# Storing finished chunks one by one and loading the next batches into their place

## Chip, cores and metric

One Trainium2 chip, one core of it. The metric is the device time of the kernel in microseconds, the median of several runs. The engines are PE (matmul), DVE (vector), ACT (scalar), POOL (general) and SP, which here issues every DMA, on one queue and in order.

## What is computed

The input `x` has 8 batches of 2048 nodes with 64 features; `adj` is a 2048 x 2048 row-normalised adjacency. Four layers follow each other, each with a residual sum and a layer normalisation over the 64 features:

```python
x = _layernorm(x + _L0_gnn_ref(x, adj, embedding, weight, bias))  # Chebyshev, K = 3, weights per node
x = _layernorm(x + _L1_gnn_ref(x, 0, net_params, adj))            # two times relu((A z) W)
x = _layernorm(x + _L2_gnn_ref(x, adj, w_self, w_neighbor, bias)) # x Ws + (A x) Wn + b
x = _layernorm(x + _L3_gnn_ref(x, adj, adj, weight, bias))        # x0, A x0, 2A(A x0)-x0, twice, then W
```

## The kernel before

**Pairs and lanes.** The 8 batches are handled as four pairs, j = 0 to 3. A pair lies in SBUF as a tensor of 128 partitions x 2048, in four chunks (c) of 512 columns. There is room for two pairs, `nat0` and `nat1`: even pairs use lane 0, odd pairs lane 1. `stg0` and `stg1` hold a second tensor of each lane, `ring` the short-lived ones, `td` is scratch in HBM.

**Passes.** A pair goes through seven products with the adjacency, passes p = 0 to 6. Passes 0 and 1 and the per-node weights are layer 0, passes 2 and 3 layer 1, pass 4 layer 2, passes 5 and 6 layer 3. Before a pass, each of its four chunks is split into a high and a low part (step `split`: ACT line 790 makes the high part, DVE line 916 the low one), since PE multiplies both (lines 652 and 653) with `B`, the adjacency's pattern. One chunk of a pass is four quarters (steps `mm`, k = 0 to 3), each of eight matmuls of 128x512. Quarter k of every chunk needs the split of chunk k of the whole tensor. After a chunk, DVE scales it (line 904), PE multiplies it with small weights (`pe_weighed`, line 670), DVE adds it to `nat` (line 945), and in passes 3, 4 and 6 the chunk is normalised (steps `centre`, `deviate`, `normed`; the last instruction of `normed` is line 965).

**Turnings.** In passes 4 and 5 a chunk must be transposed in blocks. DVE transposes within blocks (step `turn`, line 928), SP stores the result to `td` (line 1119), waits until it has landed, and loads it in another order with four DMAs (step `back`, line 1129). With k = 0 it is the tensor that goes to line 670 in that pass, with k = 1 (pass 5) the one that is split for pass 6.

**The order of work.** `order()` writes one list of steps, and every engine runs through that list and does its own part of each step. In the second half of the kernel `lane0` and `lane1` take turns: each gives the other its turn after every chunk, and also once before and once after the splits of a pass. So while one lane is at its splits, the other does up to three chunks of products in a row. Lane 0 does pair 2 and then pair 0, lane 1 pair 3 and then pair 1. Pairs 0, 1 and 2 wait after layer 0 in `zd` in HBM (step `spill`).

**The exchange.** At the end of `second(j, ...)` there are four steps `out` (line 1181), which wait for the chunk's normalisation and store the chunk. `whole_pair` of the next pair in that lane begins with one step `reload`: SP waits for all four stores of the pair before (line 1177), and loads all 2048 columns with one DMA of 1,024 KB (line 1178). Its four splits follow. In the list, `out` of pair 2 stands in pass 5 of pair 3, after the first chunk of that pass; `reload` of pair 0 and its splits stand after the second chunk of it. The exchange of lane 1 stands between pass 2 and pass 3 of pair 0, where nothing is turned. The four stores of pair 0 stand in pass 5 of pair 1, in the same way as those of pair 2.

```python
if s.kind == "reload":
    for i in range(NC):
        sp.wait_ge(s_z[n][i], 32 if j == 2 else 16)
...
    else:
        sp.wait_ge(s_out[n], 64)
    sp.dma_start(nat[n][:], zd[j]).then_inc(s_re[n], 16)
```

A second way through the same steps, for a matrix of another form, is in the program behind a flag and isn't run.

Of the kernel before, what the change touches and what calls it, by code (L numbers as in the profile page):

```python
# [17 lines left out]
NC = 4  # L18
# [16 lines left out]
Step = namedtuple("Step", "kind j p c k", defaults=(0, 0, 0, 0))  # L35
# [7 lines left out]
def order():  # L43
    steps = []

    def put(kind, *at):
        steps.append(Step(kind, *at))

    def one_pass(j, p):

        norm = p in (3, 4, 6)

        def turn(c, k):
            put("turn", j, p, c, k)

        def finish(c):
            put("after", j, p, c)
            if norm:
                if c > 0:
                    put("deviate", j, p, c - 1)  # L60
                put("centre", j, p, c)
                if c > 0:
                    put("normed", j, p, c - 1)

        order = [(c, m) for c in range(NC) for m in range(4)]
        if p == 0 or (j, p) == (2, 2):

            order[0:8] = [(0, 0), (0, 1), (1, 0), (1, 1), (0, 2), (1, 2), (0, 3), (1, 3)]
        for c, m in order:
            if p in (4, 5) and (c, m) == (0, 0):  # L70
                turn(0, 0)
            if p in (4, 5) and (c, m) == (0, 1):
                put("back", j, p, 0, 0)
            if p in (4, 5) and c < 3 and m == 2:
                turn(c + 1, 0)
            if p in (4, 5) and c < 3 and m == 3:
                put("back", j, p, c + 1, 0)
            if p == 5 and c > 0 and m == 1:
                put("back", j, p, c - 1, 1)
            put("mm", j, p, c, m)  # L80
            if c > 0 and p >= 2 and m == (3 if c == 1 and order[2] == (1, 0) else 0):
                finish(c - 1)
            if m < 3:
                yield False
                continue
            if c > 0 and p < 2:
                finish(c - 1)
            put("scale", j, p, c)
            if p == 5 and not on_pe(j, p, c):
                turn(c, 1)  # L90
            if norm and c == 3:
                put("deviate", j, p, 2)
                put("normed", j, p, 2)
            yield True
        put("after", j, p, 3)
        if norm:
            put("centre", j, p, 3)
            put("deviate", j, p, 3)
            put("normed", j, p, 3)

    def opening(j):
        put("prep2", j, 0, 0)
# [56 lines left out]
    def splits(j, p):  # L159
        for c in range(NC):  # L160
            put("split", j, p, c)
# [83 lines left out]
    def second(j, products):  # L245

        for whole in products:
            if whole:
                yield
        for p in (4, 5, 6):  # L250
            yield
            splits(j, p)
            yield
            for whole in one_pass(j, p):
                if whole:
                    yield
        for c in range(NC):
            put("out", j, 0, c)

    def whole_pair(j):  # L260
        if j < 2:
            put("reload", j)
        splits(j, 2)
        yield
        for whole in one_pass(j, 2):
            if whole:
                yield
        yield
        splits(j, 3)
        yield  # L270
        yield from second(j, one_pass(j, 3))
# [32 lines left out]
    n = 0  # L304
    while lanes[0] or lanes[1]:
        if lanes[n] and next(lanes[n], "end") == "end":
            lanes[n] = None
        n = 1 - n
# [3 lines left out]
STEPS = order()  # L312
# [1 line left out]
SECOND = STEPS.index(Step("W"))  # L314


END = STEPS.index(Step("out", 1))


def numbered(*kinds, last=False):  # L320
# [8 lines left out]
def gnn_stack(nc, xn, xt, at, rb, r16, emb, embt, b0, w01, w2, wbd, bias, eye, eps, out, zd, y1d, bd, td):  # L329
# [3 lines left out]
    with ctx:  # L333
# [18 lines left out]
        nat = [sb(f"nat{i}", [P, N], F32) for i in range(2)]  # L352
# [28 lines left out]
        def way(general):  # L381


            def sem(name):
                return ctx.enter_context(nc.semaphore(("g_" if general else "f_") + name))
# [5 lines left out]
            s_lx = [sem(f"loadx{i}") for i in range(2)]  # L391
            s_y1o = [sem(f"y1out{n}") for n in range(2)]
            s_z = [[sem(f"z{n}{c}") for c in range(NC)] for n in range(2)]
            s_re = [sem(f"reload{n}") for n in range(2)]
            s_out = [sem(f"out{n}") for n in range(2)]
            s_away = [sem(f"away{n}") for n in range(2)]
            s_back = [[sem(f"back{n}{k}") for k in range(2)] for n in range(2)]
# [5 lines left out]
            s_hi, s_evict, s_sq, s_std, s_H, s_S, s_twh = (  # L403
                sem("hi"), sem("evict"), sem("sq"), sem("std"), sem("H"), sem("S"), sem("twh"))

            s_lo, s_y, s_v, s_turn = sem("lo"), sem("y"), sem("v"), sem("turn")
# [22 lines left out]
            split_at = numbered("split")  # L429
# [24 lines left out]
            for s in STEPS:  # L454
                if s.kind == "fetch" or s.kind == "part" and s.c == 1:
                    i = s.p if s.kind == "fetch" else 1
                    n_load[i] += 32 if s.kind == "fetch" else 16
                    load_at[s], load_after[s], slot_of[s] = n_load[i], held[i], i
                    held[i] = s

            def turned(j, p, c):

# [52 lines left out]
            for s in STEPS:  # L515
                n = s.j % 2
# [28 lines left out]
            for s in STEPS:  # L545
                n = s.j % 2
# [19 lines left out]
            def ch(t, c):  # L566
                return t[:, c * 512:(c + 1) * 512]
# [61 lines left out]
            def source_of(j, p, c):  # L629

                n = j % 2
                if p == 0 and j < 2:
                    return ch(nat[n], c), s_x[c], 32
                if p == 0:
                    if c == 1:
                        return part_slot(c), s_f[1], load_at[Step("part", j, 0, c)]
                    return part_slot(c), s_p, part_at[Step("part", j, 0, c)]
                if p == 1:
                    return ch(nat[n], c), *((s_evict, evict_at[after(j, 0, c)]) if on_pe(j, 0, c) else landed(j, 0, c, 1))
                if p == 2 and j < 2:  # L640
                    return ch(nat[n], c), s_re[n], 16 * (2 - n)
                if p == 3:
                    return ch(nat[n] if j == 2 else stg[n], c), s_evict, evict_at[after(j, 2, c)]
                if p == 6:
                    return ch(stg[n], c), *((s_evict, evict_at[after(j, 5, c)]) if on_pe(j, 5, c) else landed(j, 5, c, 1))
                return ch(nat[n], c), s_norm, norm_at[Step("normed", j, {2: 1, 4: 3, 5: 4}[p], c)]
# [222 lines left out]
            def dve_steps(dv, steps):  # L869
                for s in steps:  # L870
# [58 lines left out]
                    if s.kind == "after" and p > 2:  # L929
                        dv.wait_ge(s_four, four_at[s])  # L930
                        bank = ps[:, nbank_of[s, "four"], :]
                        if p == 3:
                            if j == 3:
                                dv.wait_ge(s_norm, norm_at[Step("normed", 3, 1, c)])
                                dv.wait_ge(s_hi, split_at[Step("split", 3, 2, c)])
                            else:
                                dv.wait_ge(s_re[n], 32 if j == 0 else 16)
                                dv.wait_ge(s_hi, split_at[Step("split", j, 3 if j == 2 else 2, c)])
                            dv.scalar_tensor_tensor(v, bank, 0.0, v, ALU.max, ALU.add).then_inc(s_v, 1)
                        else:  # L940
                            if p == 6:
                                dv.wait_ge(s_v, v_at[after(j, 5, c)])
                            else:
                                dv.wait_ge(s_pb, pb_at[s])
                            dv.tensor_tensor(v, bank, v, ALU.add).then_inc(s_v, 1)  # L945
# [127 lines left out]
            def sp_settle(sp):  # L1073

                sp.wait_ge(s_here, 4)
                for n in range(2):
                    sp.wait_ge(s_out[n], 128 - 64 * n)

            def sp_rest(sp, c, v):
                for m in range(NT):  # L1080
# [17 lines left out]
            def sp_steps(sp, steps):  # L1098
                for s in steps:
# [67 lines left out]
                    if s.kind == "spill":  # L1167
                        sp.wait_ge(s_norm, norm_at[Step("normed", j, 1, c)])
                        sp.dma_start(zd[j, :, cols], ch(nat[n], c)).then_inc(s_z[n][c], 16)
                    if s.kind == "reload":  # L1170
                        for i in range(NC):
                            sp.wait_ge(s_z[n][i], 32 if j == 2 else 16)
                        if j == 2:
                            sp.wait_ge(s_hi, split_at[Step("split", 2, 3, 3)])
                            sp.wait_ge(s_lo, split_at[Step("split", 2, 3, 3)])
                        else:
                            sp.wait_ge(s_out[n], 64)
                        sp.dma_start(nat[n][:], zd[j]).then_inc(s_re[n], 16)
                    if s.kind == "out":
                        sp.wait_ge(s_norm, norm_at[Step("normed", j, 6, c)])  # L1180
                        sp.dma_start(out[j, :, cols], ch(nat[n], c)).then_inc(s_out[n], 16)
                    if s.kind == "W":
                        sp.wait_ge(s_acc, 8 * n_T)
                        sp.wait_ge(s_H, len(prep_at))
# [1 line left out]
                        sp.dma_start(W[:], wbd[:, 2:9, :]).then_inc(s_w, 16)  # L1186
                    if s == STEPS[-1]:
                        for n in range(2):
                            sp.wait_ge(s_out[n], 128)

            return Way(pe_steps, act_steps, dve_steps, pool_steps, sp_steps,
                       *((act_start, dve_start, sp_start) if general else (None, None, sp_settle)))
# [102 lines left out]
```

## Time and profile before

| | us |
|---|---|
| median of 3 runs | 1267.96 |
| lowest and highest of them | 1266.08, 1274.63 |
| the profiled execution | 1270.8 |
| its span | 1268.7 |

The rows further below come from this profiled execution. A row of a timeline has the start and the duration in us, the engine, the line, the operation with what it writes and reads, and in brackets how long the engine was idle before it and what ended that. "x4" means four instructions merged in one row, so that the duration is from the first one's start to the last one's end. Line numbers are those of the kernel before. Names such as `nat` and `ring` stand without their number.

### The profile page before, as it was taken

What the parts mean: (1) busy time and instruction counts of PE and PEld (TensorE: products, weight loads), DVE (VectorE), ACT (ScalarE), POOL (GpSimd) and SP (SyncE); (2) the same over time, 40 slices, a digit from 0 to 9 for tenths busy, and PEclk for the clock granted to TensorE, in tenths of its full rate; (3) what the DMA queues carried; (4) which work ended last, traced back from release to release, by engine and by line L of the source; (5) the groups of instructions that cost most, each with busy time, mean ns of one, the idle gap of its engine ahead of it and who ended that gap; (6) DMA issues with size and microseconds to landing.
All of it is one profiled execution on the core that took longest, in us unless ns stands there. A gap on an engine that the chain in (4) does not pass through costs nothing.

```text
span 1268.7 us, 16356 instructions
## 1 busy us (share of the span) xinstructions
PE 1232.3 (97%) x5872; PEld 1030.6 (81%) x5872; DVE 758.6 (60%) x1863; ACT 215.5 (17%) x392; POOL 62.0 (5%) x52
## 2 busy tenths in 40 slices
PE   7999999999999999999999999997999999999996
PEld 6888888788878887878888888886888888888875
DVE  5826897787777777788725654542146355544624
ACT  6622111121112101110111111100111111110110
POOL 0000000000000000000000001010000000010100
PEclk9999999999999999999999999998999999999998
DMA  9732112211111111110011143033001110330320
GB/s 346 318 100 59 38 49 64 71 50 42 46 51 62 39 38 38 30 50 13 15 34 34 30 88 67 1 98 85 1 18 50 34 34 25 84 67 9 92 59 35
DMA packets 127783, 78.16 MB, mean 62 GB/s; under 512 B 97217, under 2 KB 107969, under 8 KB 125633
## 3 DMA queue, kind: packets, MB, share of 16 engines
q1 hardware_dynamic: 127696, 77.04, 20.6%
q8 instruction: 50, 0.82, 0.3%
q14 instruction: 37, 0.30, 0.1%
HBM read 53.42 MB, written 23.59 MB: 61 GB/s over the span
## 4 chain that ended last, share of the span: by engine, by line
PE 86%; DVE 6%; DMA 3%; SPq 2%; issue 1%; ACT 1%; DVEq 0%; ACTq 0%
PE ps L652 27%; PE ps L653 27%; PE ps L756 20%; PE ps L670 7%; PE ps L691 2%; PE ps L692 2%; SPq L1129 2%; DVE nat L1018 1%; DVE ring L1018 1%; DMA td<-ring 1%; DMA raw<-in_at 1%; PE ps L664 1%; DVE xs L916 1%; DMA td<-stg 1%; DMA nat<-zd 1%
## 5 line engine op out<-in xcount | busy, mean ns | idle before, releaser
L652 PE MATMUL ps<-B,xs 128*128 128x512 f32 x1664 | 657.1, 395 | 12.2 <-DVE xs L916 12.2
L653 PE MATMUL ps<-B,xs 128*128 128x512 f32 x1664 | 650.4, 391 | 0.0
L652 PEld LDWEIGHTS ps<-B,xs 128*128 128x128 f32 x1664 | 313.6, 188 | 76.7 <-issue 10.0
L653 PEld LDWEIGHTS ps<-B,xs 128*128 128x128 f32 x1664 | 313.9, 189 | 62.4
L756 PE MATMUL ps<-Tw,xs 128*128 128x512 f32 x1280 | 309.4, 391 | 2.5 <-DVE ring L1018 2.5
L756 PEld LDWEIGHTS ps<-Tw,xs 128*128 128x128 f32 x1280 | 238.6, 188 | 55.0 <-DVE ring L1018 4.8
L904 DVE TENSOR_TENSOR ring<-ps,rrep 128x512 f32<-128x512 f32 x94 | 64.5, 689 | 245.9 <-PE ps L653 236.0
L1018 DVE SCALAR_TENSOR_TENSOR nat<-ps,embn,nat 128x128 f32<-128x128 f32 x448 | 154.0, 344 | 51.0 <-PE ps L756 50.7
L1018 DVE SCALAR_TENSOR_TENSOR ring<-ps,embn,ring 128x128 f32<-128x128 f32 x512 | 175.5, 343 | 0.0
L670 PEld LDWEIGHTS ps<-W,ring 128*128 128x128 f32 x896 | 111.6, 191 | 10.6 <-DVE ring L904 3.7
L670 PE MATMUL ps<-W,ring 128*128 128x128 f32 x896 | 113.3, 275 | 2.8 <-DVE ring L904 2.4
L945 DVE TENSOR_TENSOR nat<-ps,nat 128x512 f32<-128x512 f32 x48 | 33.1, 689 | 59.5 <-PE ps L670 59.3
L1044 POOL TENSOR_TENSOR nat<-nat,bias 128x512 f32<-128x512 f32 x32 | 41.2, 1296 | 556.7 <-DVE ring L928 556.7
L916 DVE TENSOR_TENSOR xs<-nat,xs 128x512 fp32r<-128x512 f32 x72 | 45.6, 684 | 30.9 <-ACT xs L790 30.6
L826 ACT ACTIVATE sml<-sml,epst 128x8 f32<-128x8 f32 x64 | 19.3, 301 | 234.7 <-DVE sml L960 234.7
L821 ACT ACTIVATE ps<-nat 128x512 f32<-128x512 f32 x44 | 26.5, 602 | 183.3 <-DVE nat L955 183.3
L691 PE MATMUL ps<-B,xs 128*128 128x512 f32 x128 | 52.3, 409 | 3.4 <-DVE B L878 3.4
L692 PE MATMUL ps<-B,xs 128*128 128x512 f32 x128 | 51.7, 404 | 0.0
L1018 DVE SCALAR_TENSOR_TENSOR nat<-ps,embn,ring 128x128 f32<-128x128 f32 x64 | 22.3, 348 | 46.7 <-PE ps L756 45.9
L1037 POOL TENSOR_TENSOR nat<-nat,ring 128x512 f32<-128x512 f32 x16 | 20.6, 1290 | 588.1 <-DVE ring L1018 588.1
L790 ACT CAST xs<-nat 128x512 fp32r<-128x512 f32 x72 | 39.7, 616 | 37.5 <-DMA nat<-zd 24.4
L955 DVE TENSOR_TENSOR nat<-nat,sml 128x512 f32<-128x512 f32 x64 | 44.4, 693 | 2.2
(66 smaller groups left out, 547.6 us busy)
## 6 DMA issues: line engine op xcount, KB each, us to landing
raw<-in_at SPq DMA_DIRECT2D x13, 1024.0 KB, 16.1
td<-ring SPq DMA_DIRECT2D x32, 256.0 KB, 2.1
ring<-td SPq DMA_DIRECT2D x128, 64.0 KB, 2.5
ring<-in_xn SPq DMA_DIRECT2D x16, 256.0 KB, 2.8
ring_x<-in_xt SPq DMA_DIRECT2D x32, 128.0 KB, 3.2
ring_x<-y1d SPq DMA_DIRECT2D x32, 128.0 KB, 3.3
out<-nat SPq DMA_DIRECT2D x16, 256.0 KB, 2.8
y1d<-ring SPq DMA_DIRECT2D x14, 256.0 KB, 2.7
```

Source lines behind the costliest of these rows:

```text
L652: pe.matmul(bank, x[:, 0, m, :], of, start=m == 0, stop=False)
L653: mm = pe.matmul(bank, x[:, 1, m, :], of, start=False, stop=ends and m == NT - 1)
L670: mm = pe.matmul(ps[:, bank, k * P:(k + 1) * P], src[:, k * P:(k + 1) * P], w, start=i == 0, stop=i == len(pairs) - 1)
L691: pe.matmul(bank, xs[n][:, 0, k, :], of, start=k == 0, stop=False)
L692: mm = pe.matmul(bank, xs[n][:, 1, k, :], of, start=False, stop=k == LAST)
L756: mm = pe.matmul(ps[:, 4 + 2 * p + q, :], src, Tw[:, wi, 512 * p:512 * p + 512], start=i == 0, stop=i == 4)
L790: ac.copy(part_of(j, 0, c), src).then_inc(s_hi, 1)
L904: dv.tensor_tensor(to, ps[:, bank_of["prod", j, p, c], :], ch(rrep, 0 if general else c), ALU.mult).then_inc(s_y, 1)
L916: dv.tensor_tensor(lo, src, hi.bitcast(F32), ALU.subtract).then_inc(s_lo, 1)
L955: dv.tensor_tensor(g, g, sm[:, 1, :].unsqueeze(2).to_broadcast([P, 8, C]), ALU.subtract).then_inc(s_mean, 1)
L1018: dv.scalar_tensor_tensor(sums[d % 2], ps[:, 4 + 2 * p:6 + 2 * p, i * C:(i + 1) * C], embn[:, t, d:d + 1], first[d] if d < 2 else sums[d % 2],
L1044: po.tensor_tensor(g, g, bias_t[:, p - 4, :].unsqueeze(1).to_broadcast([P, 8, C]), ALU.add).then_inc(s_pb, 1)
```

## The change

A store of pairs 0, 2 and 3 is put in the list right behind the normalisation of its chunk (`exchange`), so the first three lie within pass 6 and the fourth at its end. For pairs 2 and 3 each store but the first is followed by the reload of the chunk before it, for the pair that takes the place: 256 KB, which waits for that chunk's store alone. The reload of the fourth chunk stands where the whole reload stood. Of the four splits of pass 2 for pairs 0 and 1 the first three stay, and the fourth moves between the second and the third quarter of that pass's first chunk. Stores and reload pieces of a chunk count on the same semaphore as its `spill` (`exchanged` gives semaphore and count), so that splits and the additions of pass 3 wait for one chunk each. Pair 1's stores stay at the end. The one reload of pair 2 (from its `spill`, earlier in the kernel) is left as it was.

```diff
+        def exchange(c):
+
+            if p == 6 and j != 1:
+                put("out", j, 6, c)
+                if c > 0 and j > 1:
+                    put("reload", j - 2, 0, c - 1)
...
                 if c > 0:
                     put("normed", j, p, c - 1)
+                    exchange(c - 1)
...
+            if p == 2 and j < 2 and (c, m) == (0, 2):
+                put("split", j, 2, 3)
...
                 put("normed", j, p, 2)
+                exchange(2)
...
             put("normed", j, p, 3)
+            exchange(3)
...
-        for c in range(NC):
-            put("out", j, 0, c)
+        if j == 1:
+            for c in range(NC):
+                put("out", j, 6, c)
...
         if j < 2:
-            put("reload", j)
-        splits(j, 2)
+            put("reload", j, 0, 3)
+            for c in range(3):
+                put("split", j, 2, c)
+        else:
+            splits(j, 2)
...
+            def exchanged(j, c, back):
+
+                return s_z[j % 2][c], 16 * (3 - j % 2 + back)
...
                 if p == 2 and j < 2:
-                    return ch(nat[n], c), s_re[n], 16 * (2 - n)
+                    return ch(nat[n], c), *exchanged(j, c, 1)
...
-                                dv.wait_ge(s_re[n], 32 if j == 0 else 16)
+                                dv.wait_ge(*((s_re, 16) if j == 2 else exchanged(j, c, 1)))
...
+                    elif s.kind == "reload":
+                        sp.wait_ge(*exchanged(j + 2, c, 0))
+                        sp.dma_start(ch(nat[n], c), zd[j, :, cols]).then_inc(s_z[n][c], 16)
                     if s.kind == "out":
                         sp.wait_ge(s_norm, norm_at[Step("normed", j, 6, c)])
-                        sp.dma_start(out[j, :, cols], ch(nat[n], c)).then_inc(s_out[n], 16)
+                        sp.dma_start(out[j, :, cols], ch(nat[n], c)).then_inc(s_z[n][c] if j > 1 else s_out[n], 16)
```

On SP, at the exchange of lane 0 during pass 5 of pair 3, before:

```order
L1129 DMA ring<-td 32x16x32 x4
L1119 DMA td<-ring 128x512
L1129 DMA ring<-td 32x16x32 x4
L1119 DMA td<-stg1 128x512
L1181 DMA out<-nat0 128x512 x4
L1129 DMA stg1<-td 32x16x32 x4
L1119 DMA td<-ring 128x512
L1129 DMA ring<-td 32x16x32 x4
L1119 DMA td<-stg1 128x512
L1178 DMA nat0<-zd 128x2048
L1129 DMA stg1<-td 32x16x32 x4
```

and the same place with the change, where a turning's store has become line 1138, a `back` line 1148, a reload piece line 1197 and a store of the output line 1200:

```order
L1200 DMA out<-nat0 128x512 x2
L1197 DMA nat0<-zd 128x512
L1200 DMA out<-nat0 128x512
L1197 DMA nat0<-zd 128x512
L1138 DMA td<-ring 128x512
...
L1138 DMA td<-stg1 128x512
L1200 DMA out<-nat0 128x512
L1197 DMA nat0<-zd 128x512
L1148 DMA stg1<-td 32x16x32 x4
...
L1138 DMA td<-stg1 128x512
L1197 DMA nat0<-zd 128x512
```

Three stores and two pieces went ahead of the first turning of the pass; a store and a piece stand where four stores were; one piece stands where the whole reload was.

On DVE, at the same exchange, before (line 928 is a turning, 916 a split, 945 the addition, 904 the scale):

```order
L904 TENSOR_TENSOR ring<-ps,rrep 128x512
L928 STREAM_TRANSPOSE stg<-ring 128x512
L916 TENSOR_TENSOR xs<-nat,xs 128x512 x4
L945 TENSOR_TENSOR nat<-ps,nat 128x512
L928 STREAM_TRANSPOSE ring<-nat 128x512
L904 TENSOR_TENSOR ring<-ps,rrep 128x512
L928 STREAM_TRANSPOSE stg<-ring 128x512
L904 TENSOR_TENSOR ring<-ps,rrep 128x512
```

and with the change, where these are lines 948, 936, 965 and 924:

```order
L924 TENSOR_TENSOR ring<-ps,rrep 128x512
L948 STREAM_TRANSPOSE stg<-ring 128x512
L936 TENSOR_TENSOR xs<-nat,xs 128x512 x3
L965 TENSOR_TENSOR nat<-ps,nat 128x512
L948 STREAM_TRANSPOSE ring<-nat 128x512
L924 TENSOR_TENSOR ring<-ps,rrep 128x512
L948 STREAM_TRANSPOSE stg<-ring 128x512
L936 TENSOR_TENSOR xs<-nat,xs 128x512
L924 TENSOR_TENSOR ring<-ps,rrep 128x512
```

The fourth split moved behind the addition, the turnings and the scale of lane 1's next chunk.

## Rows read from the trace of the kernel before

**Rows 1.** The page: busy time and share of an engine.
```profile
PE 1232.3 (97%) x5872; PEld 1030.6 (81%) x5872; DVE 758.6 (60%) x1863; ACT 215.5 (17%) x392; POOL 62.0 (5%) x52
```

**Rows 2.** Waits of PE, whole span: us in total, times, longest.
```profile
PE ps L652 <- DVE xs L916: 12.2, 5, 8.0
```

**Rows 3.** Stretches: us, busy of PE, PEld, DVE, ACT, POOL, clock, DMA share, GB/s.
```profile
857.10:865.10 8.00, 0.00 (x0) 0.02 (x1) 0.83 (x2) 1.57 (x4) 0.00 (x0) 0.70 0.70 187
865.10:870.60 5.50, 5.49 (x13) 4.36 (x14) 4.18 (x7) 0.60 (x2) 1.29 (x1) 0.51 0.12 48
960.00:976.00 16.00, 16.00 (x80) 13.56 (x79) 10.96 (x21) 3.99 (x8) 0.00 (x0) 1.00 0.23 83
```

**Rows 4.** Chain that ended last, 825 to 870 us: start, us, what.
```profile
837.04 0.23 PE ps L652
...
845.68 0.46 SPq L1181
...
850.19 2.72 DMA td<-ring
...
856.37 7.13 DMA nat<-zd
863.53 0.63 ACT xs L790
...
864.27 0.70 DVE xs L916
...
865.11 0.77 PE ps L652
865.88 0.43 PE ps L653
```

**Rows 5.** Timeline of SP, lane 0's exchange.
```profile
833.51 0.33 SPq L1119 DMA_DIRECT2D td<-ring  x1
835.64 2.60 SPq L1129 DMA_DIRECT2D ring<-td  x4
...
844.53 0.63 SPq L1119 DMA_DIRECT2D td<-stg  x1
845.21 2.19 SPq L1181 DMA_DIRECT2D out<-nat  x4
847.44 2.71 SPq L1129 DMA_DIRECT2D stg<-td  x4
...
856.37 0.33 SPq L1178 DMA_DIRECT2D nat<-zd  x1
```

**Rows 6.** Timeline of DVE, same stretch.
```profile
832.17 0.69 DVE L965 TENSOR_TENSOR nat<-nat,sml 128x512 f32<-128x512 f32 x1
...
848.81 0.71 DVE L928 STREAM_TRANSPOSE stg<-ring 128x512 f32<-128x512 f32 x1
864.27 2.50 DVE L916 TENSOR_TENSOR xs<-nat,xs 128x512 fp32r<-128x512 f32 x4 [14.76 <-ACT xs L790]
```

**Rows 7.** The page: DMA issues, size of one, median us to landing.
```profile
out<-nat SPq DMA_DIRECT2D x16, 256.0 KB, 2.8
```

**Rows 8.** DMA, 833 to 842 us, in 40 slices.
```profile
GB/s 0 0 0 0 0 27 355 419 346 55 0 0 0 0 0 0 0 12 91 175 23 101 100 84 52 141 74 174 210 346 389 243 73 46 0 0 0 73 0 0
```

**Rows 9.** Timeline of PE: what waited or might have.
```profile
840.55 2.02 PE L670 MATMUL ps<-W,ring 128*128 128x128 f32 x16 [0.34 <-DMA ring<-td]
...
1193.20 2.02 PE L670 MATMUL ps<-W,ring 128*128 128x128 f32 x16
...
1223.75 0.47 PE L652 MATMUL ps<-B,xs 128*128 128x512 f32 x1 [1.47 <-DVE xs L916]
```

**Rows 10.** Timelines of SP and ACT, lane 1's exchange.
```profile
967.32 0.33 SPq L1178 DMA_DIRECT2D nat<-zd  x1
...
972.10 2.18 ACT L790 CAST xs<-nat 128x512 fp32r<-128x512 f32 x4 [3.81 <-DMA nat<-zd]
```

**Rows 11.** Chain that ended last, 1180 to 1224 us: start, us, what.
```profile
1196.38 3.17 DMA td<-stg
```

More of the change, by code:

```diff
@@ L314 @@
 SECOND = STEPS.index(Step("W"))
-END = STEPS.index(Step("out", 1))
+END = STEPS.index(Step("out", 1, 6))
 def numbered(*kinds, last=False):
@@ L393, in way @@
             s_z = [[sem(f"z{n}{c}") for c in range(NC)] for n in range(2)]
-            s_re = [sem(f"reload{n}") for n in range(2)]
+            s_re = sem("reload")
             s_out = [sem(f"out{n}") for n in range(2)]
@@ L1075, in sp_settle @@
                 sp.wait_ge(s_here, 4)
-                for n in range(2):
-                    sp.wait_ge(s_out[n], 128 - 64 * n)
+                sp.wait_ge(s_out[0], 64)
             def sp_rest(sp, c, v):
@@ L1169, in sp_steps @@
                         sp.dma_start(zd[j, :, cols], ch(nat[n], c)).then_inc(s_z[n][c], 16)
-                    if s.kind == "reload":
+                    if s.kind == "reload" and j == 2:
                         for i in range(NC):
[L1172 to L1178, printed above, removed]
+                            sp.wait_ge(s_z[n][i], 32)
+                        sp.wait_ge(s_hi, split_at[Step("split", 2, 3, 3)])
+                        sp.wait_ge(s_lo, split_at[Step("split", 2, 3, 3)])
+                        sp.dma_start(nat[n][:], zd[j]).then_inc(s_re, 16)
+                    elif s.kind == "reload":
+                        sp.wait_ge(*exchanged(j + 2, c, 0))
+                        sp.dma_start(ch(nat[n], c), zd[j, :, cols]).then_inc(s_z[n][c], 16)
                     if s.kind == "out":
                         sp.wait_ge(s_norm, norm_at[Step("normed", j, 6, c)])
-                        sp.dma_start(out[j, :, cols], ch(nat[n], c)).then_inc(s_out[n], 16)
+                        sp.dma_start(out[j, :, cols], ch(nat[n], c)).then_inc(s_z[n][c] if j > 1 else s_out[n], 16)
                     if s.kind == "W":
@@ L1188, in sp_steps @@
                         for n in range(2):
-                            sp.wait_ge(s_out[n], 128)
+                            sp.wait_ge(s_out[n], 64)
             return Way(pe_steps, act_steps, dve_steps, pool_steps, sp_steps,
```

## The prediction

> **What bounds the kernel now.** I read the engine shares first: PE is busy for 97% of the span [rows 1], so anything that does not change when PE works is worth nothing. Next the waits of PE over the whole span: before its matmuls of line 652 it stood 12.2 us in all for splits of line 916, five times, and 8.0 us of that in one piece [rows 2]. The reader is to see that this one piece is by far the largest share of it, two thirds, and the only large hole in the kernel. The table of stretches places it at 857.1 to 865.1 (PE busy 0.00), and shows what follows it: from 865.1 to 870.6 the granted clock is 0.51, half of the 2.4 GHz that the third stretch has [rows 3]. The chain of waits then says who made the hole: a matmul at full clock is 0.23 us; SP works through lane 1's turnings, comes to the whole reload of nat0 only at 856.37, and this 1,024 KB load takes 7.13 us, after which PE starts at 865.11 with matmuls of 0.43 us [rows 4]. The timeline of SP shows why it came so late: the four stores of batch pair 2 lie in one piece at 845.21, after them a back, a turning, a back, a turning, and only then the reload [rows 5]. DVE shows what was held with it: it had finished the last turning at 849.5 and stood 14.76 us until the splits [rows 6].
>
> **Part 1, the stores and reloads of lane 0 (pairs 2 to 0).** Three stores and two of four reload pieces now stand on SP before the turning of 833.51. Their data are ready early: the third chunk is normalised at 832.17 + 0.69 = 832.86 [rows 6], the first two long before. The third piece follows the last store after the turning of 844.53, the fourth stands where the whole reload stood, near 856.4 [rows 5]. The splits of chunks 0 to 2 then wait for nothing after 849.5, when DVE is done with the turning. The 8.0 us go in full, if the fourth piece is in time. PE wants its split before the fourth quarter (eight matmuls each) of the first chunk: 857.1 + 3 x 8 x 0.23 = 862.6. The piece is issued near 856.4 (a shift of this is below), lands after 2.8 us, the median of a 256 KB store of the same size, because no reload of this size is in the trace [rows 7], and the two halves of its split take 0.63 us and 0.70 us. So 856.4 + 2.8 + 0.63 + 0.70 = 860.5, two microseconds early. On DVE the moved split stands ahead only of the scale of the same chunk, which needs PE's whole chunk anyway. Gain: 8.0 us.
>
> Without the hole the clock has no reason to fall. Between 865.11 and 870.57 PE did 12 matmuls; at 0.23 us they are 2.8 us instead of 5.5 us [rows 3, 4]. Gain: 2.7 us. Could the hole be needed by something else, so that PE now meets another thing that is late? The turning of chunk 2 of lane 1 (at 868 before) was held by DVE's wait; now it goes while PE works on chunk 2, and its result is wanted only two chunks of PE after that one, each of 32 matmuls of 0.23 us, so some 15 us later. I see nothing late there.
>
> **What it costs.** SP is one queue, in order. Ahead of the first turning of pair 3's pass 5 (833.51) it now issues the third store and the second reload piece. A store's issue is 0.46 us in the chain, 0.47 with what follows it [rows 4]; the store can begin at 832.87, so the turning starts at 832.87 + 2 x 0.47 = 833.81, 0.3 us later. Then the data: the 256 KB of that turning moved in about 0.7 us (the three full slices of 0.225 us at 355, 419 and 346 GB/s) [rows 8]. Two such transfers, 1.4 us, with a head start of 0.94 us leave a backlog of 0.5 us. Together 0.8 us. From below it is 0.3 us (the backlog nothing). From above: 768 KB more cost the first reload 7.13 - 2.8 = 4.3 us, 1.44 us for 256 KB, backlog 1.9, together 2.2 us. I take 1.0 us, near the row of the same place. None of it is hidden: the result of this turning comes back at 840.55, where PE already waited 0.34 us for it [rows 9]. So PE will stand there 1.3 us. That is shorter than the 1.47 us it stood at 1223.75, after which nothing shows a lower clock [rows 9]. Loss: 1.0 us (0.3 to 2.2). It also moves PE's need and the fourth reload by the same amount, so the two microseconds above stay.
>
> In the middle of the chain SP had four stores between a turning and its return; now there are a store and a reload there, one microsecond shorter, but the return at 847.44 had to wait for its turning to land (2.7 us from 844.53 [rows 5]; another landed in 2.72 [rows 4]), so the gain there is 0.3 us at most and off the path.
>
> **Part 2, lane 1 (pairs 3 to 1).** The same exchange. The whole reload at 967.32 held ACT until 972.10 [rows 10], and PE was busy 16.00 us of 16.00 there [rows 3]. No turning stands near it on SP. Value 0, both bounds 0: there is no hole to close, and the pieces have less to wait for.
>
> **Part 3, the last stores of lane 0 (pair 0).** Three stores move ahead of the first turning of pair 1's pass 5. The third's normalisation stands on DVE right ahead of the turning, as at the other exchange, where 0.65 us lay between 832.86 and the turning's store at 833.51 [rows 5, 6]; one issue of 0.47 us is hidden in that. The backlog is 0.05 us to 0.8 us (0.7 or 1.44 us of moving, less 0.65 us of head start). The result is used at 1193.20 with no wait shown; measured by the other place (840.55 - 835.64 = 4.9 us from first return issue to use) it had hardly any slack [rows 5, 9]. Loss 0.2 us, 0 to 0.8. Later the returning of chunk 0 no longer shares with four stores: its turning took 3.17 us [rows 11]. This shortens SP's chain by 0.45 us (3.17 less the 2.72 of rows 4), but the 1.47 us stand at 1223.75 ends with a split on DVE behind an addition that needs PE; it stays [rows 9]. Pair 1's own stores at the end are unchanged. Value of the tail: 0 (0 to 0.5 gained).
>
> **Sum.** 8.0 + 2.7 - 1.0 - 0.2 = 9.5 us. The profiled execution took 1270.8 us with a span of 1268.7; it should come to 1261.3 and 1259.2. It lay 2.8 us above the median of the runs, 1267.96, so the median should be 1258.5 us, 0.75% less.
>
> **Rivals.**
> First, the added transfers are free: the turning loses only the 0.3 us of issue, or less, and the tail gives its 0.5 us. Then 10.7 - 0.3 + 0.5 = 10.9, 1257.1 us. For it: ahead of that turning the DMA engines moved nothing, the slices before it are 0 GB/s [rows 8]. Against: the turning now has half a megabyte ahead of it in its queue. With every loss below nothing and noise it would end near 1255.
>
> Second, the fourth piece is late: a piece takes as long as a whole reload took, 4.8 us [rows 10] to 7.13 us [rows 4], so that the piece ends its split at 857.4 + 4.8 to 7.1 + 1.3 = 863.5 to 865.8 while PE is there at 863.6. PE stands up to 2.2 us; 1258.5 + 2.2 = 1260.7 us. The store's 2.8 us speaks against it. The Trainium skill, page DMA: Bandwidth & Descriptors, section Bandwidth, has a rule against this change: batch transfers to 1 MiB or more. Its section on the anatomy of one DMA gives about 2.0 us fixed and the rest by size, which for 256 KB is 2.6 us, an estimate from that page for another kind of queue; by it four pieces back to back would cost three fixed parts more, and the last alone would be in time. Here three of the pieces lie far ahead, so the rule would cost nothing on PE's path.
>
> Third, on the other side: each transfer put ahead on SP's queue holds the turning behind it for a whole landing, 2.8 us, and not for its moving time. Then the first turning is 5.6 us late, PE stands 5.9 us at 840.2, and its clock falls as after the hole (2.7 us); the fourth piece is late by another 5.6 us against PE, less its two microseconds (3.6), with 2.7 us of clock again; and at 1193 another 2.8 us. Loss 5.6 + 2.7 + 3.6 + 2.7 + 2.8 = 17.4 against 10.7: 1267.96 + 6.7 = 1274.7 us. It decides for slower from a hold of about 1.9 us for each transfer on. For it: SP's chain is serial and has no slack at 840.55. Against it: the store of a turning that shared with four stores took 3.17 us, another 2.72 us [rows 4, 11]: 0.45 us for four stores, not 2.8 us for each.
>
> **How the numbers follow.** The forecast 0.66, free transfers 0.18, the late piece 0.11, the held turnings 0.05. The range is 1254.5 to 1265.5: below, the 10.9 us with 2.6 us for the spread of the runs; above, the upper bounds (1.2 + 0.6 more loss and 2.2 for the late piece) with 3 us of spread. A measurement of this kernel can tell about 1%, 12.7 us, from no change; 9.5 us lies inside. Faster by more needs all of the first rival and luck: 0.13. Slower by more only by the third: 0.04. Within: 0.83.
>
> **What would show it.** Right: PE has no wait of more than 2 us after the head, no stretch near 860 with a granted clock of 0.51; PE's wait for ring from td near 840 is 1.0 to 1.6 us; the splits of pair 0 are three and one on DVE, the three near 849.5; the span is near 1259. Wrong, if the wait of line 652 for line 916 is still over 3 us near 857 (the fourth piece, or another transfer), if the wait at 840 is over 3 us, or if the hole is gone and the span has moved by less than 6 us: then something else caught PE, and its waits would name it.

## The result, and the profile after

| | before | with the change |
|---|---|---|
| median, us | 1268.78 (14 runs) | 1261.64 (14 runs) |
| lowest to highest | 1266.08 to 1274.63 | 1259.77 to 1266.56 |
| the profiled execution | 1270.8 | 1260.2 |
| its span | 1268.7 | 1258.2 |

The ratio is 0.994, with a 95% interval of 0.9928 to 0.9953: 0.6% faster, between 6.0 and 9.1 us. The medians are 7.1 us apart. The forecast was 1258.5 us (0.75% less), with a range of 1254.5 to 1265.5: right in sign, mechanism and range, 2.4 us too hopeful in what is gained (9.5 forecast, 7.1 measured). It had also said that a gain of this size could not be told from no change; with 14 runs of each it can.

The waits of PE over the whole span (us in total, times, longest) answer to [rows 2]. Lines 652, 670, 916 and 945 of before are now 672, 690, 936 and 965.

```profile
PE ps L672 <- DVE xs L936: 4.2, 4, 1.5
...
PE ps L690 <- DMA ring<-td: 1.8, 1, 1.8
```

The wait for splits has lost one of its five parts, and with it 8.0 of 12.2 us. The wait for returned turnings has grown to 1.8 us. The same stretches as in [rows 3] show PE busy through all of them, at the full clock:

```profile
857.10:865.10 8.00, 8.00 (x37) 6.64 (x36) 2.71 (x4) 0.62 (x1) 0.00 (x0) 1.00 0.47 102
865.10:870.60 5.50, 5.50 (x34) 4.85 (x33) 0.78 (x2) 0.00 (x0) 0.00 (x0) 1.00 0.42 95
...
960.00:976.00 16.00, 16.00 (x79) 13.48 (x78) 9.33 (x18) 1.72 (x4) 0.00 (x0) 1.00 0.00 1
```

The timeline of SP around lane 0's exchange answers to [rows 5] (line 1138 stores a turning, 1148 returns it, 1200 stores a finished chunk, 1197 loads a piece):

```profile
831.52 0.33 SPq L1200 DMA_DIRECT2D out<-nat  x1
831.90 0.43 SPq L1197 DMA_DIRECT2D nat<-zd  x1
832.38 0.46 SPq L1138 DMA_DIRECT2D td<-ring  x1
836.07 2.61 SPq L1148 DMA_DIRECT2D ring<-td  x4
...
843.83 0.62 SPq L1138 DMA_DIRECT2D td<-stg  x1
844.50 0.43 SPq L1200 DMA_DIRECT2D out<-nat  x1
844.97 0.46 SPq L1197 DMA_DIRECT2D nat<-zd  x1
846.59 2.61 SPq L1148 DMA_DIRECT2D stg<-td  x4
...
855.16 0.43 SPq L1197 DMA_DIRECT2D nat<-zd  x1
```

The first turning's store is issued at 832.38 and its return can begin only at 836.07, 3.7 us later; before it was 833.51 and 835.64, 2.1 us. DVE and PE show both ends of this (line 948 is a turning, 936 a split, 965 the addition, 924 the scale):

```profile
831.42 1.30 DVE L948 STREAM_TRANSPOSE ring<-nat 128x512 f32<-128x512 f32 x2
...
849.55 1.85 DVE L936 TENSOR_TENSOR xs<-nat,xs 128x512 fp32r<-128x512 f32 x3
851.78 0.69 DVE L965 TENSOR_TENSOR nat<-ps,nat 128x512 f32<-128x512 f32 x1 [0.38 <-PE ps L690]
...
859.62 0.69 DVE L936 TENSOR_TENSOR xs<-nat,xs 128x512 fp32r<-128x512 f32 x1 [0.94 <-ACT xs L810]
...
864.49 0.69 DVE L924 TENSOR_TENSOR ring<-ps,rrep 128x512 f32<-128x512 f32 x1 [4.18 <-PE ps L673]
```

```profile
840.66 2.02 PE L690 MATMUL ps<-W,ring 128*128 128x128 f32 x16 [1.81 <-DMA ring<-td]
```

The reader is to see three things: three splits right behind the turning, where DVE before stood 14.76 us [rows 6]; the fourth split, ready at 860.3; and the scale of that chunk at 864.49, so its fourth quarter began eight matmuls of 0.23 us earlier, at 862.6. The fourth piece had 2.3 us to spare.

### The profile page after: what moved, and what is told of

It is laid out like the page before. It is cut to its first block, busy times and chain, and to the rows that moved or that the text cites. A ratio compares the mean times of both kernels' runs of the same rounds, so it can differ in the third digit from the quotient of the medians.

```text
span 1258.2 us, 16358 instructions
## 1 busy us (share of the span) xinstructions
PE 1228.9 (98%) x5872; PEld 1028.3 (82%) x5872; DVE 758.8 (60%) x1863; ACT 215.5 (17%) x392; POOL 62.0 (5%) x52
## 4 chain that ended last, share of the span: by engine, by line
PE 90%; DVE 6%; DMA 2%; issue 1%; SPq 1%; ACT 1%; DVEq 0%; ACTq 0%
PE ps L672 29%; PE ps L673 29%; PE ps L776 20%; PE ps L690 8%; PE ps L711 2%; PE ps L712 2%; DVE nat L1038 1%; DVE ring L1038 1%; DMA raw<-in_at 1%; PE ps L684 1%; DVE xs L936 1%; DVE sml L980 0%; SPq L1080 0%; ACT xs L810 0%; DVE sml L971 0%
## 5 line engine op out<-in xcount | busy, mean ns | idle before, releaser
L975 DVE TENSOR_TENSOR nat<-nat,sml 128x512 f32<-128x512 f32 x64 | 44.4, 693 | 2.2
L985 DVE TENSOR_TENSOR nat<-nat,sml 128x512 f32<-128x512 f32 x64 | 44.3, 692 | 2.2
```

Source lines behind the costliest of these rows:

```text
L975: dv.tensor_tensor(g, g, sm[:, 1, :].unsqueeze(2).to_broadcast([P, 8, C]), ALU.subtract).then_inc(s_mean, 1)
L985: dv.tensor_tensor(g, g, sm[:, 0, :].unsqueeze(2).to_broadcast([P, 8, C]), ALU.mult).then_inc(s_norm, 1)
```

## The experiments

All kernels were timed against the kernel before, those of one group on one chip. The theory: the gain is the hole of lane 0's exchange and the half clock behind it, less what the transfers ahead of one turning cost. The rivals are that the gain sits elsewhere, and that the missing 2 us (7.1 in the medians, 9.2 by 8.0 + 2.7 - 1.5 from the two traces) are a cost I don't see. The two profiled spans themselves lie 10.5 us apart; 0.9 us of that is a wait of PE near 20 us, where the change does nothing (3.4 us before, 2.5 us with the change, 2.1 to 3.5 us over all traces).

### Both kernels profiled again

No edit: the kernel before, and the changed one.

> The kernel before, profiled a second time. Theory A (hole 8.0 us, then 2.7 us of half clock, both in every run): the wait of line 652 for line 916 near 857 is again 7.5 to 8.5 us and the stretch behind it has a granted clock near 0.5. Theory B (part of the 10.7 us belongs to the one profiled execution): the hole or the half clock behind it is shorter by about 2 us, or the start of the kernel accounts for the difference. Time within 0.3% of before.

> The changed kernel, profiled a second time. Both theories: ratio 0.993 to 0.9955. A: PE's wait for ring from td near 840 is again 1.6 to 2.0 us. B would allow it to be over 3 us here, which would explain the missing 2 us of the medians (7.1 us gained against 9.2 us by the two traces).

The kernel before against itself gave 0.9988 (0.9974 to 1.0002), which is how well a ratio here can be known. The change gave 0.9937 (0.9918 to 0.9956), median 1261.82. The chain of the second profile of before:

```profile
853.80 5.14 DMA nat<-zd
858.97 0.63 ACT xs L790
859.71 0.70 DVE xs L916
860.55 0.77 PE ps L652
861.32 0.43 PE ps L653
```

and its waits of PE, whole span:

```profile
PE ps L652 <- DVE xs L916: 9.1, 5, 4.9
```

The whole reload took 5.14 us and not 7.13 us, and the hole was 4.9 us and not 8.0 us. The half clock was there again, for 12 matmuls. In the second profile of the change PE waited 1.7 us near 840:

```profile
PE ps L690 <- DMA ring<-td: 1.7, 1, 1.7
```

So theory B holds: the first profile had caught a long reload. Its spread is seen again in two of the next kernels, which keep the whole reload at its old place. The second profile of before also shows PE waiting 1.1 us near 839 for the first turning, against 0.3 us in the first: with nothing ahead of it on SP, that turning took 3.25 us from its issue to its return (831.29 to 834.54), and not 2.1 us.

```profile
839.11 2.02 PE L670 MATMUL ps<-W,ring 128*128 128x128 f32 x16 [1.11 <-DMA ring<-td]
```

### One lane at a time

```diff
-            if p == 6 and j != 1:
+            if p == 6 and j in EARLY:            # lane 0 only: (2,); lane 1 only: (0, 3)
                 put("out", j, 6, c)
-                if c > 0 and j > 1:
+                if c > 0 and j in PIECES_OF:     # (2,); (3,)
                     put("reload", j - 2, 0, c - 1)
```

with the whole reload and four splits together in the other lane, as before.

> Only the exchange of lane 0 (pair 2 to pair 0) is done chunk by chunk; lane 1's exchange and the stores of pair 0 are as before. Theory (all of the gain is the hole of lane 0's exchange): ratio to before as of the whole change, 0.994, within 0.001; the hole is gone, the wait near 840 is 1.8 us. Rival (the other parts carry a part, by fewer transfers in the way at the end): ratio 0.996 or more.

> Only the exchange of lane 1 (pair 3 to pair 1) and the early stores of pair 0; lane 0's exchange as before. Theory: nothing gained, ratio 0.999 to 1.001; the hole near 857 is 8 us as before. Rival (the early stores shorten SP's chain near the end): 0.5 us or more gained, and PE's 1.5 us wait near 1223 shrinks.

Lane 0 alone gave 0.9935 (0.9913 to 0.9957), the whole gain. Lane 1 and pair 0 gave 0.999 (0.9971 to 1.0009), nothing. Its hole was the longest of all: the chain, then the waits of PE.

```profile
856.24 8.29 DMA nat<-zd
```
```profile
PE ps L678 <- DVE xs L942: 13.7, 5, 9.5
```

Near the end it kept the 1.5 us wait of before, so the shorter row of stores there is worth nothing that the ratio can tell, as the forecast had it.

### Early stores, whole reload

```diff
 PIECES_OF, EARLY = (), (0, 2, 3)
```

> Stores of pairs 0, 2 and 3 go right behind their chunks, but each reload is whole and stands where it stood. Theory (the reload's place and size make the hole, not the stores): the hole near 857 is 7 to 8 us, ratio 0.999 to 1.001; the wait near 840 is 0.3 to 1.1 us, with one transfer ahead of the turning. Rival (the four stores in one piece are what delays the reload): the reload is issued 1.5 us or more earlier and the hole shrinks by as much.

0.9994 (0.9976 to 1.0013): nothing. The chain and the waits of PE:

```profile
854.70 5.31 DMA nat<-zd
```
```profile
PE ps L678 <- DVE xs L942: 10.4, 5, 6.2
...
PE ps L696 <- DMA ring<-td: 0.2, 1, 0.2
```

The hole was 6.2 us, a little under what was expected, again with a reload of another length. From the first turning's store to the reload it is 22.7 us here and 22.5 to 22.9 us in the three traces with the four stores in a row, so that row did not delay the reload. And with one store, but no piece, ahead of the turning, PE's wait at 840 is 0.2 us (this row is that wait): a lone store costs nothing there. The traces of the two other kernels with nothing ahead of the turning, lane 1 only and the one of the next section, show no wait there at all.

### Pieces at the old place

```diff
-            put("reload", j, 0, 3)
-            for c in range(3):
+            for c in range(NC):
+                put("reload", j, 0, c)
+            for c in range(4):
                 put("split", j, 2, c)
```

with the stores in a row as before, and no split moved.

> Stores as before, each reload cut in four pieces that are issued one after the other where the whole one stood, all four splits ahead of the products. PE needs only the first piece to begin. Theory: the first piece lands 2.8 to 3.5 us after its issue instead of 7.1 us, so the hole shrinks from 8.0 to about 4 us and the clock may still fall; ratio 0.996 to 0.998. Rival (cutting costs as much as it gives, four landings in a row): hole still 7 us or more.

0.9984 (0.9967 to 1.0001), median 1267.94. The chain and the waits:

```profile
857.02 4.02 DMA nat<-zd
```
```profile
PE ps L669 <- DVE xs L933: 9.3, 5, 5.1
```

The first of four pieces issued in a row took 4.0 us, against 5.1 to 8.3 us of a whole one, and left a hole of 5.1 us, inside what the whole load leaves (4.9 to 9.5). The ratio stands for 2 us, its interval for anything from nothing to 4 us. What the cut alone is worth at this place stays open; it is less than the place.

### The whole load at an early place

```diff
             exchange(3)
+            if (j, p) == (2, 6):
+                put("reload", 0, 0, 0, 1)        # the whole of nat0, one DMA
```

with early stores, no pieces, and four splits together.

> Stores right behind their chunks, and the reload of pair 0 in one DMA of 1,024 KB, but issued right behind the last store, near 845, and all four splits together. It waits for the last store to land (2.3 us) and holds SP meanwhile. Theory (the place of the load makes the hole, not its size): landed by about 854, splits done before 857, hole gone, wait near 840 under 1 us, ratio 0.993 or lower. Rival (the large load is in the way of the returns behind it, so size matters): a wait for ring or stg from td of over 1 us near 850 to 860, ratio 0.995 or more.

Median 1259.18, ratio 0.9931 (0.9909 to 0.9954). The timeline of SP, then of ACT:

```profile
843.11 0.43 SPq L1212 DMA_DIRECT2D out<-nat  x1
846.10 0.32 SPq L1206 DMA_DIRECT2D nat<-zd  x1
```
```profile
851.38 2.19 ACT L818 CAST xs<-nat 128x512 fp32r<-128x512 f32 x4 [10.02 <-DMA nat<-zd]
```
```profile
PE ps L698 <- DMA ring<-td: 0.6, 1, 0.6
```

The last row is PE's only wait from 800 to 1000 us. One load of 1,024 KB, issued eight to ten microseconds earlier (846.10 against 853.8 to 856.4), removes the hole as well as four pieces do, though SP stands 2.5 us for the last store and the returns go beside the load. So the rival fell: at a place with time enough, the size is not what matters. With nothing ahead of the first turning but one store, it also avoids most of the change's own loss.

### What stands ahead of the turning

Three kernels move the same transfers. The first puts two behind the first turning's store:

```diff
             if p in (4, 5) and (c, m) == (0, 0):
                 turn(0, 0)
+                if (j, p) == (3, 5):
+                    put("out", 2, 6, 2)
+                    put("reload", 0, 0, 1)
```

> As the change, but the third store and the second reload piece of lane 0 go on SP's queue behind the first turning's store of pair 3's pass 5 and ahead of its return, where SP waits for the landing anyway. Theory (the 1.5 us longer wait near 840 is the backlog of the two transfers ahead of that turning): the wait falls from 1.8 us to 0.3 to 0.8 us and the time is 1.0 to 1.5 us below the change's, ratio to before 0.993. Rival (any transfer in flight beside the turning lengthens it): the wait stays at 1.5 us or more, and the time stays.

Median 1259.97 (1258.7 to 1260.93), ratio 0.9922 (0.9904 to 0.9941), where the change itself in the same group had 1261.82 (1260.46 to 1263.28). SP, answering to the rows of the change above:

```profile
832.01 0.33 SPq L1141 DMA_DIRECT2D td<-ring  x1
832.38 0.43 SPq L1203 DMA_DIRECT2D out<-nat  x1
832.85 0.46 SPq L1200 DMA_DIRECT2D nat<-zd  x1
834.24 2.61 SPq L1151 DMA_DIRECT2D ring<-td  x4
```

The turning lands in 2.2 us instead of 3.7, and between 830 and 846 us PE waits for nothing. The median is 1.8 us lower, and the wait that is gone was 1.8 us. The second kernel puts the two transfers one place later, behind the return:

```diff
             if p in (4, 5) and (c, m) == (0, 1):
                 put("back", j, p, 0, 0)
+                if (j, p) == (3, 5):
+                    put("out", 2, 6, 2)
+                    put("reload", 0, 0, 1)
```

> As the kernel that put the third store and the second piece behind the first turning's store, but one place later, behind its return. Theory: the wait near 840 is 0.3 to 0.6 us, now with nothing beside the return, but the second turning starts 0.9 us and more later; its result has some 2 us to spare, so time as that kernel, ratio 0.992 within 0.001. Rival (SP's chain has no slack further on): a new wait for ring from td near 850 of 0.5 us or more and a time above it.

Median 1260.13, ratio 0.9931 (0.9916 to 0.9945): the same within what can be told. The rival's new wait for a return did not come, nor did one at 840, but SP's chain was later by what it issued, and the fourth piece with it (855.93, where PE now came to its fourth quarter at 861.0): PE's only wait between 800 and 1000 us is

```profile
PE ps L675 <- DVE xs L939: 0.6, 1, 0.6
```

The third puts all five early transfers right ahead of the turning:

```diff
+            if p == 6 and j == 2 and c < 2:
+                return
+            if p == 6 and (j, c) == (2, 2):
+                for i in range(3):
+                    put("out", j, 6, i)
+                put("reload", 0, 0, 0)
+                put("reload", 0, 0, 1)
+                return
```

> As the change, but all three early stores and both early reload pieces of lane 0 stand right ahead of the first turning of pair 3's pass 5: five transfers of 256 KB instead of two. Theory (a transfer ahead holds the turning for issue and moving, about 0.7 us each beyond a head start): the wait near 840 grows from 1.8 us by 3 x 0.7 = 2.1 us to 3.5 to 4.5 us, time 2 us above the change. Rival (each holds it for a whole landing of 2.3 to 2.8 us): the wait is over 8 us, and the clock falls.

Median 1263.95, ratio 0.9953 (0.9935 to 0.9971). That is 2.1 us over the change's median, which was taken in another group; by the ratios it is 1.6 to 2.0 us, and their intervals overlap. PE at the place, and the stretch behind it (us, busy of PE, PEld, DVE, ACT, POOL, clock, DMA share, GB/s):

```profile
842.37 2.62 PE L698 MATMUL ps<-W,ring 128*128 128x128 f32 x16 [3.93 <-DMA ring<-td]
```
```profile
842.40:846.00 3.60, 3.60 (x19) 3.38 (x20) 0.98 (x2) 0.00 (x0) 0.00 (x0) 0.67 0.25 42
```

3.9 us, in the range of the theory (3.5 to 4.5), far from the over 8 us of whole landings. But it came out right by another sum than mine. SP:

```profile
827.34 4.11 SPq L1208 DMA_DIRECT2D out<-nat  x2
831.49 0.93 SPq L1205 DMA_DIRECT2D nat<-zd  x2
832.47 0.43 SPq L1146 DMA_DIRECT2D td<-ring  x1
837.52 2.61 SPq L1156 DMA_DIRECT2D ring<-td  x4
```

SP is ahead of the list, so the first two stores went as soon as their chunks were normalised, here too. What stood in the turning's way beyond the change was one load, not three transfers, and it took the landing from 3.7 to 5.1 us: 1.4 us for one load, and 2.1 us of wait. The half clock did come, from 843.6 to 847.0, after a wait of 3.9 us; by the starts of the matmuls, set beside those of the change, it cost 1.6 us. Wait and clock are 3.7 us more than in the trace of the change, whose span is 3.3 us shorter.

### The fourth split and the fourth piece

First the split moved back to the other three:

```diff
-            for c in range(3):
+            for c in range(4):
                 put("split", j, 2, c)
...
-            if p == 2 and j < 2 and (c, m) == (0, 2):
+            if False:
```

> As the change, but the fourth split stays with the other three, ahead of lane 1's next chunk on ACT and DVE. Its piece of the reload is issued near 855.2 and lands near 858.7, so DVE waits at that split from 851.5 to 859.4 and holds the addition, a turning and the scale of pair 3 behind it. Theory: PE begins pair 0's first chunk in time, since only the later quarters need that split; but the turning of pair 3's fourth chunk and the scale come 2 us late. PE meets the scale's result only after its next chunk, so the time is that of the change within 1 us (0.993 to 0.995). Rival (what is held on DVE reaches PE): a wait of 1 us or more between 857 and 870, ratio 0.9955 or more.

Median 1261.91, ratio 0.9949 (0.9931 to 0.9966); the change's 0.994 lies inside. DVE stood there and held what was behind:

```profile
859.70 0.69 DVE L936 TENSOR_TENSOR xs<-nat,xs 128x512 fp32r<-128x512 f32 x1 [6.94 <-ACT xs L810]
860.31 0.68 DVE L965 TENSOR_TENSOR nat<-ps,nat 128x512 f32<-128x512 f32 x1
```

The addition came 8.5 us later than in the change (851.78), and PE had no wait between 842 and 1000. So the moved split is worth nothing that can be measured here; what it protects has slack. Then the piece, one return later:

```diff
             if p == 5 and c > 0 and m == 1:
                 put("back", j, p, c - 1, 1)
+                if (j, c) == (3, 2):
+                    put("reload", 0, 0, 3)
```

and its old place left empty for pair 0.

> As the change, but the fourth piece of pair 0's reload is issued one return later, near 859.8 instead of 855.2. Theory (it has 2.3 us to spare): it lands near 863.3 and its split is ready near 864.8, PE is there at 862.6, so PE waits about 2 us before the fourth quarter, time 2 us above the change, clock not lowered. Rival (no slack was left or more than I think): wait over 4 us, or none.

Median 1264.82, ratio 0.9967 (0.9955 to 0.9978), about 3 us over the kernel with the split unmoved, in the same group, and over the change. The chain:

```profile
860.00 3.54 DMA nat<-zd
...
863.56 0.63 ACT xs L813
...
864.31 0.70 DVE xs L939
...
865.15 0.77 PE ps L675
865.92 0.43 PE ps L676
```

A wait of 2.8 us, and the half clock behind it for seven matmuls (865.15 to 868.37, 3.2 us for what takes 1.6). The place was as expected and the slack nearly so (a wait of some 2 us was expected); that the clock would stay up was wrong.

## Why the prediction was right, and where its size was off

**The hole: right in kind, 8.0 us was one draw.** Lane 0's exchange alone carries the whole gain, and both ways of loading early remove it. But the term was taken from a single trace in which the reload took 7.13 us. In four traces with a whole reload at the old place (the two of before, lane 1 only, early stores) it took 7.13, 5.14, 8.29 and 5.31 us, and the hole was 8.0, 4.9, 9.5 and 6.2 us, mean 7.2. The step that was mis-sized is "Gain: 8.0 us".

**The half clock: right, a little less than 2.7 us.** There is a stretch of it behind each of the four holes. From the first matmul behind the hole to the fourteenth it is 5.54, 5.51, 4.99 and 5.66 us. At the full clock, behind the 0.6 us wait in the kernel with two transfers behind the return, it is 3.06 us. So the half clock cost 2.5, 2.5, 1.9 and 2.6 us, mean 2.4.

**The turning: right in kind, 1.0 us was too little.** The issue of two transfers cost 0.23 us (from DVE's start to the store 0.96 us, before 0.73), as worked out (0.3). The backlog was 3.7 - 2.1 = 1.6 us by the two first profiles, where the row of the same place gave 0.5 and the upper bound 1.9. Over all traces, the turning took 3.7 to 3.8 us with the two transfers ahead (five traces) and 2.1, 2.2, 2.2 and 3.25 us with none, so 1.3 us on average. Only the waits say how much reached PE: 1.8 us in the profile of the change against 0.3, 1.7 in its second against 1.1. The sign that the prediction had named, a wait of 1.0 to 1.6 us, was just missed. A store alone ahead costs nothing (0.2 us in the kernel with early stores), and one load more in the heap cost 1.4 us, so the reload piece is the part that holds; a piece without a store was not tried. The view of [rows 8] for the change, 829 to 842 us in slices of 0.325 us, shows how it went:

```profile
GB/s 359 139 183 38 132 69 145 63 0 0 246 403 277 164 158 158 277 315 252 227 19 0 0 0 0 3 118 81 101 67 114 120 107 295 395 202 13 0 0 0
```

From the eleventh slice on, the store, the piece and the turning move together for eleven slices, 3.5 us, with one slice only at the pace (355 to 419 GB/s) from which I had taken 0.7 us for each: it is 1.2 us each. A store and the turning alone, in the kernel with early stores, do keep that pace: 831 to 836 us in slices of 0.125 us, some 512 KB in thirteen slices, 0.8 us each.

```profile
GB/s 0 0 0 0 0 0 0 0 0 180 426 393 426 442 344 459 360 459 311 311 82 66 0 0 0 0 0 0 0 0 0 0 0 0 0 0 31 62 175 169
```

So the step that was mis-sized is the moving time of 0.7 us for each of the two transfers: it was read from a store and used for a load too. Why a load and two stores together move more slowly is not shown. With the two behind the turning's store the loss is gone.

**Sum again.** 7.2 + 2.4 - 1.5 (a wait of 1.9 us on average of the five traces with both transfers ahead, less 0.4 of the four traces above) = 8.1 us, inside 6.0 to 9.1. In one of the five traces, the split unmoved, the clock also fell behind this wait, which cost 1.6 us there, 0.3 us on average: 7.8 us. The medians' 7.1 us is 0.7 us lower; that is no more than one ratio here can tell, and I have nothing that names it.

**Lane 1 and the tail: right.** Nothing that can be told, by the one-lane kernels. The traces show two small things that went against each other. The ten traces with pair 0's early stores have a wait for a turning near 1183 of 0 to 0.5 us (0 and 0.3 in the two of the change), about the forecast 0.2 us, and the four without them have none there. Those four have a wait for a turning near 1215 of 0, 0.2, 0.8 and 1.5 us, which none of the ten has.

**The rivals.** The free transfers were wrong: they cost some 1.5 us. The late piece did not come (2.3 us to spare, 2.0 worked out), but two kernels made it come, with 0.6 and 2.8 us. The 2.8 us that the piece was to take, from the stores, was too little: the pieces took 3.5 us (median of eight in the change). The Trainium skill's rule of 1 MiB batches (page DMA: Bandwidth & Descriptors, section Bandwidth) did not decide here: the one large load at an early place did as well as four pieces, and the four at the late place no worse than one. The three fixed parts more, worked out for four pieces back to back, are not seen: all four were in SBUF 6.2 us after the first was issued, where a whole load took 5.1 to 8.3 us. The third rival's hold of a whole landing for each transfer did not come: the two together made the turning 1.3 to 1.6 us later where it wanted 5.6, and PE waited 1.8 us where it wanted 5.9.

**A version that beats both.** Two transfers behind the first turning's store (median 1259.97, 1.8 us below the change in the same group). The whole reload behind the last store had 1259.18, in another group; the two can't be told apart.

## What to carry to other kernels

When a load makes the critical engine wait, look first at where it stands in its queue and only then at how large it is: here eight to ten microseconds earlier was worth the whole gain, a cut into four at the same place 2 us, which is not told from nothing. Transfers moved forward must not go ahead of a small one that someone is already waiting for; put behind its issue, where the queue waits for its landing anyway, they cost nothing that the one trace of it shows. The next place back made the fourth piece 0.6 us late. And a stall that ends with a DMA should be priced from several traces, not one.

## What the hardware showed that I had not expected

The same load of 1,024 KB at the same place took 5.1, 5.3, 7.1 and 8.3 us in four traces, with the same neighbours in SP's queue, and why is not shown. The load of lane 1's exchange, with no turning beside it, took 4.7 or 4.8 us in the three traces looked at (both of before, early stores). And the waits after which the granted clock falls are shorter than I thought: after 1.81 us of waiting sixteen small matmuls took 2.02 us, after 2.01 us, in the kernel with the split unmoved, 2.53 us, with a granted clock of 0.77 in that stretch (840.3 to 843) and of 0.50 from 842 to 845, and after 2.8 us seven of the large ones ran at half the clock. One and the same wait of about 2 us can go either way: 2.05 us in the kernel with lane 0 only left those sixteen at 2.02.

```profile
840.39 2.53 PE L690 MATMUL ps<-W,ring 128*128 128x128 f32 x16 [2.01 <-DMA ring<-td]
```

This row, from the timeline of PE in that kernel, is to be read beside the 2.02 us of the row at 840.66 in the change.
